# The last stage's preparation moved into earlier stages, and TensorE multiplying the identity at four places where it waits

## The reference, cut to what matters

```python
x = x + L0_ffn(L0_cond(x, ...))                # per-sequence matrix; gated feed-forward, layer norm
x = x + L1_ffn(L1_cond(x, ...))                # gated unit with adapters, down projection; mixture 1
x = x + L2_ffn(L2_cond(x, ...))                # qkv, paged attention, output projection; mixture 2
w = weights[subjects]                          # L3_cond: 32x32 per sequence
c = einsum('bct,bcd->bdt', x, w)
x = x + einsum('bsd,od->bso', c, W) + bias + einsum('ebsr,eor,e->bso', xa, Bf, coeffs * scales)
```

## Time and profile before

| | |
|---|---|
| median of 3 runs | 3490.33 us (3486.12 to 3491.93) |
| the profiled execution | 3486.69 us, its span 3484.9 us |
| TensorE busy | 3303.1 us, 95% of the span; mean granted clock 0.976 |
| VectorE, ACT, GpSimd busy | 2325.4, 1764.9, 1369.3 us (67%, 51%, 39%) |
| DMA | 571.95 MB, 164 GB/s on the mean |
| stages that the diff touches | down projection from 755.9, mixture 1 from 937, attention from 1668, output projection from 2937.2, mixture 2 from 3300, last stage from 3396.1 |

### The profile page before, as it was taken

How to read it: one execution, slowest core, us unless ns; L and a number is a source line. 1 busy time by engine, 2 the same in 40 slices (tenths; PEclk the granted TensorE clock), 3 DMA queues, 4 the chain that set the end, 5 groups by cost and what they waited for, 6 DMA issues and landing times. The chain is left out here.

```text
span 3484.9 us, 69495 instructions
## 1 busy us (share of the span) xinstructions
PE 3303.1 (95%) x22214; PEld 3048.6 (87%) x22214; DVE 2325.4 (67%) x6609; ACT 1764.9 (51%) x4303; POOL 1369.3 (39%) x2426
## 2 busy tenths in 40 slices
PE   7799799999989999999799999989999998999988
PEld 5688699988878888888799999989999998888877
DVE  6444444445457777778888888888888886322274
ACT  4322222233227778788566666656666665322212
POOL 0221100000017878888556555555555552100022
PEclk9899899999999999999899999999999999999999
DMA  5410532234545555556766666656666666533333
GB/s 204 131 59 26 135 95 81 74 113 130 187 160 162 181 168 179 183 173 206 230 215 218 210 216 216 208 181 207 214 215 213 211 216 195 177 109 109 109 124 124
DMA packets 456501, 571.95 MB, mean 164 GB/s; under 512 B 171657, under 2 KB 341449, under 8 KB 439242
## 3 DMA queue, kind: packets, MB, share of 16 engines
q1 hardware_dynamic: 436426, 429.08, 39.5%
q0 software_dynamic: 19712, 138.42, 11.3%
HBM read 394.60 MB, written 172.75 MB: 163 GB/s over the span
## 5 line engine op out<-in xcount | busy, mean ns | idle before, releaser
L2316 PE MATMUL l2a_x<-l2a_pt,l2a_V 128*128 128x128 f32 x4096 | 542.5, 275 | 4.4 <-DVE l2a_pn L2257 3.6
L2316 PEld LDWEIGHTS l2a_x<-l2a_pt,l2a_V 128*128 128x128 f32 x4096 | 503.2, 193 | 5.0 <-issue 4.9
L2234 DVE CUSTOM_DVE_ANT_0 l2a_sm<-l2a_s,l2a_B 128x544 f32<-128x544 f32 x512 | 369.6, 722 | 92.6 <-PE l2a_s L195 80.4
L1479 POOL TENSOR_TENSOR moe_xr<-moe_xr,moe_bias 128x512 f32<-128x512 f32 x32 | 42.1, 1318 | 960.7 <-DMA moe_xr<-s_x 960.6
L2184 ACT ACTIVATE l2a_p<-l2a_sm,l2a_st 128x544 f32<-128x544 f32 x512 | 379.8, 742 | 27.9 <-DVE l2a_st L2237 27.6
L2043 POOL CAST l2a_K<-cache 128x256 fp32r x768 | 294.4, 433 | 223.4 <-issue 223.4
L2043 POOL CAST keys<-cache 128x256 fp32r x750 | 298.4, 447 | 188.2 <-issue 112.0
L2170 ACT ACTIVATE l2a_pt<-l2a_t 128x512 f32<-128x512 f32 x512 | 305.6, 597 | 128.3 <-PE l2a_t L2302 128.0
L2302 PE MATMUL l2a_t<-ident,l2a_p 128*128 128x128 f32 x2048 | 336.1, 287 | 5.4 <-ACT l2a_ao L2177 5.4
L2302 PEld LDWEIGHTS l2a_t<-ident,l2a_p 128*128 128x128 f32 x2048 | 288.4, 210 | 6.5 <-issue 5.9
L2248 DVE TENSOR_SCALAR l2a_p<-l2a_p,l2a_st 128x512 f32<-128x512 f32 x512 | 280.8, 548 | 18.2
(11 more groups left out here) (766 smaller groups left out, 8715.1 us busy)
## 6 DMA issues: line engine op xcount, KB each, us to landing
s_qT<-l2q_qo SPq DMA_DIRECT2D x128, 512.0 KB, 2.9
head<-s_qT SPq DMA_DIRECT2D x64, 512.0 KB, 5.8
l2a_Q<-s_qT SPq DMA_DIRECT2D x64, 512.0 KB
s_ao<-l2a_ao SPq DMA_DIRECT2D x64, 512.0 KB, 4.9
l2o_a<-s_ao SPq DMA_DIRECT2D x128, 256.0 KB, 3.0
s_kn<-l2q_ko SPq DMA_DIRECT2D x128, 128.0 KB, 3.1
head<-s_kn SPq DMA_DIRECT2D x32, 512.0 KB, 6.0
l2q_stage<-in_wqkv SPq DMA_DIRECT2D x32, 384.0 KB, 4.1
```

Of the source, the lines that this page charges most:

```text
L1479: pool.tensor_tensor(xr[tt][:, :], xr[tt][:, :], bias[:, :], ALU.add).then_inc(biased, 1)
L2234: dve.tensor_tensor_reduce(out=smr[sc % 2][:, :], in0=ps_s[sc % 2][:, 224:768], in1=Br[g % 2][:, :], scale=1.0, scalar=-3e38, op0=ALU.add, ...
L2316: pe.matmul(px[:, P:256], V[:, k * D + hg * P:k * D + hg * P + P], pt[:, k, :], start=k == 0, stop=False)
```

## The change

- `keep_busy` multiplies the 128x128 identity by itself, in float32, into a part of PSUM that nobody reads: 22 times at the start of `l1_down`, 30 times at that of `l2_out`, and in attention ahead of the scores of units 1, 2, 4 and 256 (15, 8, 10, 30 times) and of the value products of unit 248 (15 times), the last two behind a wait for an ACT copy.
- The bias in both mixtures is added by VectorE (`with_bias`), one tile ahead, behind `parts`; GpSimd has no program there.
- `Blocks` runs in `l2_out` (column block 2, first 16 steps) instead of in the second mixture; it uses the weights' staging buffers, and `o` has 4 slots instead of 8.
- `Fold`, new, runs beside the second mixture: it loads the factors and matrices of the last stage, makes `a3`, `b3`, the product, `base`, and loads and splits the first three token tiles.
- `l3` starts with its tiles and has none of that.

```diff
+def keep_busy(pe, out, turn, n):
+
+
+    for _ in range(n):
+        pe.matmul(out, turn, turn, start=True, stop=True)
...
+            keep_busy(pe, pw[7][:, 0:P], ident[:, :], 22)
             for cb in range(4):
...
 class Blocks:
...
+    def mask(self, dve, m):
+        if m == 0:
+            self.w.ready_to(dve, len(self.w.tiles) - 1)
+            dve.wait_ge(self.wg_in, 16 * NB)
+            dve.wait_ge(self.jm_in, 16)
+        for j in range(4):
+            dve.tensor_scalar(self.wx(m)[:, :, j, :], self.wg[:, 4 * m:4 * m + 4, :], self.jm[:, j:j + 1], None,
+                              ALU.mult).then_inc(self.masked, 1)
+
+    def high(self, act, m):
+        act.wait_ge(self.masked, 4 * m + 4)
+        act.activation(self.bd[0][:, 4 * m:4 * m + 4, :, :], self.wx(m), ACT.Copy).then_inc(self.hi, 1)
+
+    def low(self, dve, m):
+        dve.wait_ge(self.hi, m + 1)
+        low_part(dve, sl(self.bd, S_, slice(4 * m, 4 * m + 4), S_, S_), self.wx(m)).then_inc(self.lo, 1)
...
+class Fold:
...
+    def late(self, sp, tt, stores):
+        if tt == 1:
+            sp.dma_start(self.whole[:, :, :], rows_of(self.A["base3"], 0, 4)).then_inc(self.whole_in, 16)
+        if 6 <= tt < 9:
+            t = tt - 6
+            sp.wait_ge(*stores.landed(t, 2))
+            sp.dma_start(self.xn[t][:, :], self.src[t * P:(t + 1) * P, :]).then_inc(self.xn.sem(t), 16)
 
     def on_scalar(self, act, tt):
-        if 2 <= tt < 6:
-            m = tt - 2
-            gs = slice(4 * m, 4 * m + 4)
-            act.wait_ge(self.masked, 4 * m + 4)
-            act.activation(self.bd[0][:, gs, :, :], self.wx[:, gs, :, :], ACT.Copy).then_inc(self.hi, 1)
+        if tt == 2:
+            act.wait_ge(self.a_in, 16)
+            act.activation(self.a3[0][:, :, :], self.araw[:, :, :], ACT.Copy).then_inc(self.a_hi, 1)
+        if tt == 3:
+            act.wait_ge(self.cw_set, 1)
+            act.wait_ge(self.b_in, 16)
+            for k in range(2):
+                act.activation(self.braw[:, k, :], self.braw[:, k, :], ACT.Copy, scale=self.cw[:, k:k + 1]).then_inc(self.b_scaled, 1)
+        if tt == 4:
+            act.wait_ge(self.b_scaled, 2)
+            act.activation(self.b3[0][:, :, :], self.braw[:, :, :], ACT.Copy).then_inc(self.b_hi, 1)
+        if 8 <= tt < 11:
+            t = tt - 8
+            act.wait_ge(*self.xn.landed(t, 1))
+            act.activation(self.xh[t][0][:, :], self.xn[t][:, :], ACT.Copy).then_inc(self.x_hi, 1)
+        if tt >= 12:
+            k = tt - 12
+            act.wait_ge(self.folded, k + 1)
+            act.activation(self.base[0][:, k, :], self.whole[:, k, :], ACT.Copy).then_inc(self.base_hi, 1)
+
+    def on_vector(self, dve, tt, banks):
+        if tt == 1:
+            dve.wait_ge(self.cf_in, 16)
+            dve.wait_ge(self.sc_in, 16)
+            dve.tensor_tensor(self.cw[:, :], self.cf[:, :], self.sc[:, :], ALU.mult).then_inc(self.cw_set, 1)
+        if tt == 4:
+            dve.wait_ge(self.a_hi, 1)
+            low_part(dve, sl(self.a3, S_, S_, S_), self.araw[:, :, :]).then_inc(self.a_lo, 1)
+        if tt == 6:
+            dve.wait_ge(self.b_hi, 1)
+            low_part(dve, sl(self.b3, S_, S_, S_), self.braw[:, :, :]).then_inc(self.b_lo, 1)
+        if 9 <= tt < 12:
+            t = tt - 9
+            dve.wait_ge(self.x_hi, t + 1)
+            low_part(dve, sl(self.xh[t], S_, S_), self.xn[t][:, :]).then_inc(self.x_lo, 1)
+        if 12 <= tt < 16:
+            k = tt - 12
+            if k == 0:
+                dve.wait_ge(self.whole_in, 16)
+            dve.wait_ge(self.fold_mm, k + 1)
+            dve.tensor_tensor(self.whole[:, k, :], self.whole[:, k, :], banks[k][:, :], ALU.add).then_inc(self.folded, 1)
+        if tt >= 13:
+            k = tt - 13
+            dve.wait_ge(self.base_hi, k + 1)
+            low_part(dve, sl(self.base, S_, k, S_), self.whole[:, k, :]).then_inc(self.base_lo, 1)
+
+    def on_tensor(self, pe, tt, banks, weighed):
+
+        k = tt - 11
+        if 0 <= k < 4:
+            if k == 0:
+                pe.wait_ge(self.a_lo, 1)
+                pe.wait_ge(self.b_lo, 1)
+            pe.wait_ge(weighed, 13 + k)
+            mm3(pe, banks[k][:, :], [(sl(self.a3, S_, m, slice(k * P, (k + 1) * P)), sl(self.b3, S_, m, S_))
+                                     for m in range(2)]).then_inc(self.fold_mm, 1)
...
 def moe(nc, A, S, before, kind, Beside):
...
+                beside.late(sp, tt, xr)
...
-        @block.gpsimd
-        def _(pool):
-            pool.wait_ge(bias_in, 16)
-            for tt in range(NT):
-                pool.wait_ge(*xr.landed(tt, 1))
-                pool.tensor_tensor(xr[tt][:, :], xr[tt][:, :], bias[:, :], ALU.add).then_inc(biased, 1)
 
...
+            def with_bias(tt):
+                if tt < NT:
+                    dve.wait_ge(*xr.landed(tt, 1))
+                    dve.tensor_tensor(xr[tt][:, :], xr[tt][:, :], bias[:, :], ALU.add).then_inc(biased, 1)
...
+            dve.wait_ge(bias_in, 16)
+            with_bias(0)
             for tt in range(NT):
...
                 parts(tt + 4)
-                if tt > 1:
-                    next(side, None)
-                    next(side, None)
+                with_bias(tt + 1)
+                beside.on_vector(dve, tt, pl)
+            beside.on_vector(dve, NT, pl)
...
                 lora(tt + 1)
+                beside.on_tensor(pe, tt, pl, weighed)
...
+    fill = {1: 15, 2: 8, 4: 10, U // 2: 30}
...
+                    if sc in fill:
+                        if sc > LV:
+                            pe.wait_ge(o_copied, sc - LV)
+                        keep_busy(pe, ps_x[1][:, 0:P], ident[:, :], fill[sc])
...
+                    if pv == U // 2 - 8:
+                        pe.wait_ge(o_copied, pv)
+                        keep_busy(pe, ps_x[1][:, 0:P], ident[:, :], 15)
...
-    o = st.slots("o", 8, [P, D])
+    o = st.slots("o", 4, [P, D])
...
+                if cb == 2 and k % 4 == 2 and k < 16:
+                    blocks.high(act, k // 4)
...
+                if cb == 2 and k % 4 == 0 and k < 16:
+                    blocks.mask(dve, k // 4)
+                if cb == 2 and k % 4 == 3 and k < 16:
+                    blocks.low(dve, k // 4)
...
+            keep_busy(pe, acc[1][3][:, 0:P], ident[:, :], 30)
             for n, (cb, k) in enumerate(steps):
...
-            sp.dma_start(cf[:, :], A["coef"]).then_inc(cf_in, 16)
-            sp.dma_start(sc[:, :], A["scal"]).then_inc(sc_in, 16)
-            sp.dma_start(braw[:, :, :], rows_of(A["bt3"], 0, 2)).then_inc(braw_in, 16)
-            sp.dma_start(araw[:, :, :], rows_of(A["a3n"], 0, 2)).then_inc(a3_in, 16)
-            tokens(0)
-            tokens(1)
-            sp.dma_start(whole[:, :, :], rows_of(A["base3"], 0, 4)).then_inc(base_in, 16)
+            tokens(3)
...
-            pe.wait_ge(a_lo, 1)
-            pe.wait_ge(b_lo, 1)
-            for k in range(4):
-                if k >= 2:
-                    pe.wait_ge(folded, k - 1)
-                mm3(pe, pm[k % 2][:, :], [(sl(a3, S_, m, slice(k * P, (k + 1) * P)), sl(b3, S_, m, S_)) for m in range(2)]).then_inc(fold_mm, 1)
-            pe.wait_ge(bd_made, 4)
...
-                if tt == 0:
-                    pe.wait_ge(base_lo, 4)
```

More of the change, by code:

```diff
@@ L1357, with __init__ @@
 class Blocks:
-    def __init__(self, st, A, S):
-        self.A = A
+    def __init__(self, st, A, S, w):
+        self.A, self.w = A, w
         self.bd = S["bd"]
@@ L2332, in l2_out @@
     acc = [[st.ps(f"acc{j}{i}", [P, D]) for i in range(4)] for j in range(2)]
-    o = st.slots("o", 8, [P, D])
+    o = st.slots("o", 4, [P, D])
+    blocks = Blocks(st, A, S, w)
     a_hi, a_lo, out_mm, copied = (st.sem(n) for n in ("a_hi", "a_lo", "out_mm", "copied"))
@@ L2431, in _ @@
                     low(n)
-            for n in range(N):
+            for n, (cb, k) in enumerate(steps):
                 low(n + 3)
                 weights(n + 6)
+                if cb == 2 and k % 4 == 0 and k < 16:
+                    blocks.mask(dve, k // 4)
+                if cb == 2 and k % 4 == 3 and k < 16:
+                    blocks.low(dve, k // 4)
         @block.tensor
         def _(pe):
+            keep_busy(pe, acc[1][3][:, 0:P], ident[:, :], 30)
             for n, (cb, k) in enumerate(steps):
@@ L2457, in l3 @@
     st = Stage(nc, "l3")
-    base = st.pair("base", [P, 4, D])
-    whole = st.sb("whole", [P, 4, D])
-    araw = st.sb("araw", [P, 2, D])
-    a3 = st.pair("a3", [P, 2, D])
-    b3 = st.pair("b3", [P, 2, D])
-    bd, bd_made = S["bd"], S["bd_made"]
-    base_in, a3_in = st.sem("base_in"), st.sem("a3_in")
-    bias, bias_in = st.const("bias", [P, D])
-    cf, cf_in = st.const("cf", [P, 2])
-    sc, sc_in = st.const("sc", [P, 2])
-    braw, braw_in = st.const("braw", [P, 2, D])
-    cw, cw_set = st.const("cw", [P, 2])
-    NX = 8
-    xn = st.slots("xn", NX, [P, D], each=2)
-    xh = [st.pair(f"xh{i}", [P, D]) for i in range(4)]
+    base, bd = S["base3"], S["bd"]
```

(25 more changed lines are left out.)

85 lines of the change are left out of this document (39 added, 46 removed).

## The result

The changed kernel took 3461.94 us in the median of 4 runs (3459.59 to 3466.44), the kernel before 3490.82 beside it: ratio 0.9921, 95% interval 0.9904 to 0.9939, some 27.5 us faster. The forecast was 3473 with a range from 3464 to 3483: the sign is right, the gain is larger than forecast by about half.

What follows compares the result with a forecast made beforehand. TensorE was taken to bound nearly everything, at half clock after handovers, with a chain of waits in the last stage; -14.1 + 0.2 + 0.5 - 2.5 - 1.2 - 0.3 = -17.4 us gave 3473 us, range 3464 to 3483.

Steps and rivals of the forecast that it cites:

- parts 2 and 3: Second and first mixture: GpSimd additions and `Blocks` go, bias and fold come; net +0.2 us and +0.5 us.
- the +0.5: First mixture: net us from the bias on VectorE (+2.2) and the GpSimd collisions that go (1 to 3), bounds -1.5 and +2.2.
- part 3: First mixture: 0.60 us more in VectorE's loop makes the cadence 5.08 us instead of 4.88, +2.2 us in 12 tiles.
- The sign "4.9 to 5.1 in both": Both mixtures: `moe_xr` sums 4.9 to 5.1 us apart would show the forecast right.
- the 3.6 us: Whole kernel: the runs' median, 3490.33 us, lies this far above the profile's like; the same step was added to 3469.3.
- within 6: Last stage: the first `l_po` within 6 us of the stage's first load would show the forecast right.
- The working to the first `po`: Last stage: one `pc`, ACT's high part, VectorE's low part and waking up put the first `po` 3.2 us after the stage.
- Rival A: Last stage: TensorE's clock stays up into it, 4.3 us more gain, 3468.6 us; chance 0.18.
- rival B: Identity multiplications don't hold the clock and end late themselves: only 7.0 us gained, 3483.3 us; chance 0.08.
- the term of 2.5 us: Output projection: 30 identities keep the clock up for the first two steps; 2.5 us less, limited by the split ending at 2954.88.
- The wait for `l1d_a7L`: Down projection, second column block: this wait, 1.75 us before, would grow to over 4 us, taking back the identities' gain.
- 2.7 was reckoned: Down projection: 22 identities keep the clock up, worth 2.7 us, which come back as waiting in the second column block.

Runs made afterwards that it cites:

- the second trace: The changed kernel run again, unedited: 3465.14 us in 5 runs, ratio 0.9927 to the kernel before.
- the kernels of 3456.77 and 3455.34 us: Changed kernel with the added identities that paid and reordered down projection loads, 3456.77 us; the same with output projection weights' low parts on VectorE alone, 3455.34 us.

## Why the prediction was off

**The whole.** The mean of the two ratios is 0.9924, 26.5 us; the forecast was 17.4. Forecast and measured by stage, the latter as differences of the table's means over the traces with the same code in that stage:

```
                       forecast   measured
down projection            0      not told from 0
mixture 1                +0.5     -4.0  (94.5 to 90.5)
attention                -1.5     -2.4
output projection        -2.5     -0.5
mixture 2 to last sum    -1.7     -2.5  (98.4 to 95.9)
last stage, with tail   -12.2    -14.9  (87.8 to 72.9)
```

They sum to 24.3; the other 2.2 us are within what two executions differ by.

**The step that failed** is the price of the collisions of GpSimd's additions with VectorE, in parts 2 and 3: 1.9 us in mixture 2 and "1 to 3" in mixture 1. The direction was right, the size was not. The prediction named the rule of the Trainium skill (SBUF — State Buffer), found "a few" stretched rows, and kept to one operation's minimum and maximum. But the rows were there: going through every VectorE line of the two mixtures in the trace of before and adding up each duration less the shortest of its kind (same line, operation and shape) gives 7.4 and 9.1 us, in 19 stretched instructions, where the same sum in the trace after is some 0.5 in each. One such line, before and after:

```profile
L1547 DVE TENSOR_SCALAR moe_sm<-moe_sm x16: 230/231/1290, 942.8 to 1019.8; 128x8 f32<-128x8 f32 x16
```

```profile
L1650 DVE TENSOR_SCALAR moe_sm<-moe_sm x16: 230/231/232, 940.9 to 1016.5; 128x8 f32<-128x8 f32 x16
```

A median of 231 hides it. Some 3.3 us of each sum lie ahead of the mixture's first sum, where four or five tokens' bias additions come close together and TensorE waits for VectorE. From the last matmul of the down projection to the first sum mixture 1 took 20.6, 24.3, 19.4 and 21.8 us with the bias on GpSimd, and 17.5 to 19.0 in all kernels in which GpSimd adds nothing. In two of the four (24.3 and 21.8) a second stretch of half clock, 3.4 us long, lies in that time (at 956.1 and at 947.2); no trace with the bias on VectorE has one there. Whether the collisions bring it about was not tested.

What came back in mixture 1 was the 4.0 us and, on top, the 2.0 that the bias now costs there (next paragraph): some 6 us where the +0.5 had counted on 1.7. In mixture 2 moving the bias was worth 2.5 us (moved alone) to 3.2 (moved back), its cost included, where 1.4 were counted.

**The cost of the bias on VectorE** was right, by the loop of part 3. In mixture 1 the sums from the third to the thirteenth are 5.09 us apart after, 5.25 and 4.91 in turn at first, where the prediction said 5.08. In the trace of before they are 5.00 apart, but 4.88 without the gap of 6.46 (and the one behind it) in which an addition of 1.30 us on GpSimd stretches a subtraction at 1001.77 us to 1.52. That is 2.0 us in ten tiles. In mixture 2 without the fold the sums are 4.88 apart, so the bias costs nothing there (0.5 was counted), and with it 4.5 to 6.4. The sign "4.9 to 5.1 in both" held in mixture 1 on the mean, and not in mixture 2.

**The base of the sum.** The forecast set its terms against one trace. That trace had the cheapest mixture 1 and the cheapest last stage of those with this code (92.4 of 92.4 to 96.4, 86.6 of 86.6 to 89.6). In the last stage two of five fell to half clock a second time. Moving the sum by the 3.6 us to the median kept the terms as they were, and that was wrong: part of what lay between the trace and the median is what the change removes. Against the mean of its like the trace was cheaper by 2.1 us in mixture 1, 0.8 in mixture 2 and 1.2 in the last stage, so some 4 of the 9 us that the forecast missed were the luck of one trace.

**The last stage** was foreseen well in its mechanism: the first `po` starts 5.2 us after the first load (3390.62), within 6, and the clock is at half for 10.2 us. The working to the first `po` has slips: its four parts make 2.8 us and not 3.2, and two `pc` stand ahead of it, not one. In the kernel with more identities, at full clock, it takes 2.94 us. Against the kernel with the old last stage, 13.3 us are gained where 12.2 were counted. Rival A did not happen; the experiments show what it was worth, 73.4 less 68.9 or 4.5 us, where the prediction said 4.3.

**The identities** hold the clock, so rival B is out: 1.00 over 60 and 44 records of them. In the output projection the term of 2.5 us was mis-sized for three reasons. In the first trace the data came 2.24 us after the last identity and the clock fell anyway, 1.5 us after TensorE had resumed:

```profile
2932.62 6.94 PE L203 MATMUL l2o_acc<-ident 128*128 128x128 f32 x60 [1.17 <-PEq L2168]
...
2941.80 0.47 PE L195 MATMUL l2o_acc<-l2o_as0H,l2o_woH 128*128 128x512 f32 x1 [2.24 <-DVE l2o_as0L L207]
```

It fell in three of the seven traces with 30 identities, those with a gap of 2.24, 2.25 and 2.33 us; it stayed up behind 1.65, 1.75 and 1.82, and behind 2.31 too. In the second trace, where it did not fall, the fourth step waited 1.85 us for the stretched split shown above. The prediction had bounded the gain by the split that ended at 2954.88; it ends at a later point of the stage in some executions (20.4 us after attention's last product against 19.1), and then less is left. And the trace of before had more half clock behind its first product there than others without identities: 5.8 us against 3.9, 5.4 and 3.4.

**The down projection.** The wait for `l1d_a7L` did not grow to over 4 us; the waiting is spread over others:

```profile
802.94 0.50 PE L195 MATMUL l1d_pw<-l1d_a4H,l1d_wdH 128*128 128x512 f32 x1 [1.19 <-DVE l1d_a4L L207]
...
807.70 0.50 PE L195 MATMUL l1d_pw<-l1d_a8H,l1d_wdH 128*128 128x512 f32 x1 [0.87 <-DVE l1d_a8L L207]
809.11 0.50 PE L195 MATMUL l1d_pw<-l1d_a9H,l1d_wdH 128*128 128x512 f32 x1 [0.45 <-DVE l1d_a9L L207]
...
811.84 0.39 PE L195 MATMUL l1d_pw<-l1d_td0H,l1d_bd0H 128*128 128x256 f32 x1 [0.62 <-DVE l1d_td0L L207]
```

The mechanism held in kind: between the two first profiles the first block gained 2.6 us (2.7 was reckoned) and the second gave 1.6 of them back, and the new half clock at 929.2 took 1.5 more at the stage's end. In the changed kernel's second trace the second block gave back all. More can't be told from traces that spread by 3 us in this stage.

**Attention** gained 2.4 us rather than 1.5, and the difference lies in its middle: up to the scores of unit 240 the traces with identities are 0.3 us ahead, as forecast, and from there to unit 280 another 2.1, where 1.2 were counted.

**Left open.** The calls in attention were not tried one at a time, and what ends the waits of the down projection's second block was changed only together with identities (the kernels of 3456.77 and 3455.34 us).

## What to carry to other kernels

Before pricing an operation on GpSimd, add up, over all VectorE lines of the stage, what each instruction takes beyond the shortest of its kind; a median hides it. Here 16.5 us were found so, and a third to a half of them (5.2 to 8.7 us) came back when the operation moved, net of its cost on VectorE. Moving such an operation to VectorE can pay even where VectorE is the busier engine. Where TensorE idles at a handover, multiplications that nobody needs pay if they end just before the data come (4.5 us in the last stage, with 0.53 us left idle of 3.43) and if TensorE, not a load or a split, bounds what follows (0 to 1 us in the mixtures). Take the base of a sum from two or three traces of the same kernel: one may be lucky in exactly the stage that is changed.

## What was not expected of the hardware

- 32 additions of 1.04 us on GpSimd, for which nothing waits, make the kernel 11.2 us slower; 32 writes of 0.52 us can't be told from none.
- A VectorE operation on 8 columns is stopped by a GpSimd write that only writes SBUF (0.57 us for 0.23), where a 128x512 subtraction beside such a write takes its usual 0.68.
- The granted clock fell to 0.50 for 3.4 us, 1.5 us after TensorE had resumed at full clock (2943.3 against 2941.80): the idle 2.24 us lay before that.
- Executions of one kernel in the same conditions spread by 18 us before the change (3483.0 to 3500.8 in 8 runs) and by 9 after (3460.08 to 3469.03 in 5).
